# Three interaction layers of a recommendation tower: 24 of 39 fields multiplied in pairs, seven block products for eight

## The reference

```
prev = x
for k in 0, 1, 2:
    z = einsum('bmd,bhd->bdmh', x, prev)          # all products of a field and a unit
    t = einsum('bdc,co->bdo', z, w[k]) + b[k]     # 128 outputs
    t = t / sqrt(sum of t*t over outputs and d)   # one norm per sample
    logit.append(t); prev = t
z = sum over d of the three t                     # 384 numbers per sample
h = relu([z, dense] @ W_top1 + b_top1); h = relu(h @ W_top2 + b_top2); y = h @ W_top3
```

## Time and profile before

| | us |
|---|---|
| median of 3 runs (1243.51 to 1246.41) | 1246.39 |
| the profiled execution, its time | 1242.94 |
| its span, first to last instruction | 1240.9 |
| TensorE busy | 1201.1 |
| VectorE busy | 877.9 |
| GpSimd busy | 157.5 |
| ScalarE busy | 81.6 |

### The profile page before, as it was taken

One profiled execution on the slowest core, in us unless ns is written; L12 is line 12 of the kernel. 1 busy time (PEld: TensorE's weight loads), 2 busy tenths in 40 slices (PEclk: granted clock), 3 DMA queues, 4 the chain that ended last, 5 costly groups with the idle time before them and its releaser, 6 DMA issues.

```text
span 1240.9 us, 9676 instructions
## 1 busy us (share of the span) xinstructions
PE 1201.1 (97%) x2808; PEld 531.4 (43%) x2808; DVE 877.9 (71%) x748; ACT 81.6 (7%) x139; POOL 157.5 (13%) x183
## 2 busy tenths in 40 slices
PE   0899999999999999999999999999999999999999
PEld 0334444444444444444444444444444444444443
DVE  1657787677687777768678677867767876876671
ACT  0010010101001010000101000010100001010002
POOL 5130203020030301103030120303002030000000
PEclk9899999999999999999999999999999999999999
DMA  4988275461826647183563718356271745627000
GB/s 96 400 247 298 58 248 148 176 216 58 280 62 223 172 152 226 50 287 76 196 200 126 233 39 281 111 177 218 100 245 50 260 135 177 215 69 260 0 1 0
DMA packets 92574, 203.70 MB, mean 164 GB/s; under 512 B 41756, under 2 KB 49692, under 8 KB 92567
## 3 DMA queue, kind: packets, MB, share of 16 engines
q1 hardware_dynamic: 85786, 202.08, 49.6%
q0 software_dynamic: 5120, 1.29, 1.3%
q10 hardware_dynamic: 1660, 0.25, 0.1%
HBM read 201.67 MB, written 1.90 MB: 164 GB/s over the span
## 4 chain that ended last, share of the span: by engine, by line
PE 93%; SPq 4%; DMA 1%; POOL 1%; issue 1%; DVE 0%; ACT 0%; POOLq 0%
PE acc L464 84%; PE acc L448 7%; SPq L218 1%; SPq L188 1%; SPq L210 1%; POOL gathered L167 1%; PE t_ps L515 1%; SPq L203 1%; DMA xr<-xt 1%; DMA xt<-gathered 0%; PE acc L505 0%; PE nrm_ps L474 0%; DMA gathered<-in_table,rows_of 0%; SPq L190 0%; DMA base_sb<-in_base 0%
## 5 line engine op out<-in xcount | busy, mean ns | idle before, releaser
L464 PE MATMUL acc<-z,w_sb 128*128 128x512 f32 x2496 | 1079.6, 593 | 6.8 <-DVE z L353 6.7
L353 DVE TENSOR_TENSOR z<-t_ps,xb 128x1536 f32<-128x1536 f32 x416 | 709.0, 1752 | 227.8 <-PE acc L464 142.1
L464 PEld LDWEIGHTS acc<-z,w_sb 128*128 128x128 f32 x2496 | 473.5, 190 | 597.9 <-issue 571.4
L167 POOL DMA_INDIRECT gathered<-in_table,rows_of x160 | 152.8, 955 | 60.8 <-issue 47.8
L448 PE MATMUL acc<-xr,w_sb 117*128 117x512 f32 (+1 forms) x224 | 102.6, 609 | 29.3 <-issue 28.6
L161 POOL TENSOR_TENSOR rows_of<-ids_sb,base_sb 128x10 int32<-128x10 int32 x16 | 3.3, 205 | 795.4 <-DMA xt<-gathered 793.9
L339 DVE TENSOR_TENSOR xr<-x,xr 117x512 f32<-117x512 f32 (+1 forms) x112 | 69.0, 686 | 31.4 <-DMA x<-xt 18.3
L448 PEld LDWEIGHTS acc<-xr,w_sb 117*128 117x128 f32 (+1 forms) x224 | 43.3, 195 | 85.4 <-issue 82.9
L378 DVE RECIPROCAL inv<-root 128x96 f32<-128x96 f32 (+2 forms) x18 | 12.4, 687 | 60.9 <-ACT root L292 60.8
L280 ACT ACTIVATE t_ps<-acc,bias 128x512 f32<-128x512 f32 x16 | 10.6, 662 | 461.1 <-PE acc L464 421.2
L268 ACT ACTIVATE sq<-scaled,bias 128x512 f32<-128x512 f32 x16 | 11.6, 722 | 387.8 <-issue 268.8
(11 more groups left out here) (41 smaller groups left out, 53.6 us busy)
## 6 DMA issues: line engine op xcount, KB each, us to landing
xb<-xt SPq DMA_DIRECT2D x208, 768.0 KB, 6.3
xr<-xt SPq DMA_DIRECT2D x144, 156.0 KB
x<-xt SPq DMA_DIRECT2D x45, 78.0 KB
gathered<-in_table,rows_of POOLq DMA_INDIRECT x160
xr<-xt SPq DMA_DIRECT2D x32, 78.0 KB
w_sb<-in_w SPq DMA_DIRECT2D x13, 192.0 KB, 10.3
xt<-gathered SPq DMA_DIRECT2D x16, 72.0 KB, 6.9
wt_sb<-in_wt SPq DMA_DIRECT2D x1, 768.0 KB
```

Source lines behind the costliest of these rows:

```text
L167: nc.gpsimd.indirect_dma_start(gathered[0:n, g, :], None, table[:, :], bass.IndirectOffsetOnAxis(rows_of[0:n, g:g + 1], 0)).then_inc(rows_ ...
L353: nc.vector.tensor_tensor(z[:, s % ZSLOTS, :, :], fields_of(k), xb[:, c * CH:(c + 1) * CH, :], ALU.mult).then_inc(z_ready, 1)
L464: last = nc.tensor.matmul(acc[k][:, :], w_sb[k][:, m, :], z[:, s % ZSLOTS, r, :], start=(m == 0), stop=(m == FIELDS - 1))
```

## The change

Two fields a and b, whose weights are cut into left and right halves of outputs (64 each) and whose z is cut into two halves of columns (N1, N2, 256 each, samples 0 to 15 and 16 to 31 of the tile), form a 2x2 by 2x2 block product. Strassen's scheme (in Winograd's form) does it with seven block products of 128 rows, 64 outputs and 256 columns in place of eight, and with sums before and after. 24 of the 39 fields are paired (12 pairs, two pairs to a chunk "P" of 4 fields, 6 such chunks a layer); 15 stay direct, three to a chunk "D". A layer is D P P D P P D P P D D, 11 chunks. What changes:

- **TensorE.** Every matmul of layers 0 to 2 and of the norms has 64 outputs, LEFT (PSUM partitions 0 to 63) or RIGHT (64 to 127). A direct field is two of them with 512 columns. A P chunk is 14 blocks of 256 columns: 8 that need only z and weights, 2 that need the first sum, 4 that need the others. Three of the seven products go to accumulators shared by pairs (`mix_ps`, `p7_ps`). The order of a tile is as before, with `range(0, 5)` before `add_partitions` and `range(5, 11)` after it.
- **GpSimd.** Per P chunk three adds or subtracts of 128x512 (`pair_sums`), into two slots; per tile three of 128x48 (`mix_rows`), which form the sign-changed and mixed rows of x that the scheme needs (so z itself comes out already combined); the gathers are split 8 and 2 and stand behind the last P chunk of layers 1 and 2.
- **VectorE.** Products of 3 rows (D) or 4 rows (P), into a ring of 14 rows; four sums of weights per layer, once (`mixed_weights`); per layer and tile five sums of 64x256 (`shared_sums`) and an add to the accumulator (`add_shared`); layer 0's seven products in four instructions. `normalize` stands after chunk 4, `scale0` after chunk 5.
- **ScalarE.** Per layer three copies between partition halves (`carry`); layer 1's bias moves to VectorE.
- **SyncE.** The mixed rows go to DRAM (`xq`) and each P chunk of `xb` is two loads; w1 is loaded whole at the start; the dense layers' weights are loaded into `xb` at the end.

The core of the diff (the ring, semaphores, buffers and the adapted norms are left out):

```diff
+CHUNKS = [("D", 0), ("P", 0), ("P", 1), ("D", 1), ("P", 2), ("P", 3), ("D", 2), ("P", 4), ("P", 5), ("D", 3), ("D", 4)]
+LEFT, RIGHT = slice(0, UNITS // 2), slice(UNITS // 2, UNITS)
+N1, N2 = slice(0, H), slice(H, N)
...
+            def pair_sums(i, k, c):
...
+                b11, t3 = z[:, at:at + 2, N1], z[:, at:at + 2, N2]
+                b21, b22 = z[:, at + 2:at + 4, N1], z[:, at + 2:at + 4, N2]
+                t2, t4, t1 = (sums[:, n % SUM_SLOTS, r, :, :] for r in range(3))
+                pool.wait_ge(z_ready, chunks_to(i, k, c))
...
+                nc.gpsimd.tensor_tensor(t2, t3, b11, ALU.add).then_inc(sums_ready, 1)
+                pool.wait_ge(sums_ready, done + 1)
+                nc.gpsimd.tensor_tensor(t4, b21, t2, ALU.subtract).then_inc(sums_ready, 1)
+                nc.gpsimd.tensor_tensor(t1, b22, t2, ALU.subtract).then_inc(sums_ready, 1)
...
+            def tile(i, mix=True, gathers=True, last=False):
...
+                        pair_sums(i, k, c)
+                        if k == 1 and c == FIRST_P and mix:
+                            mix_rows(i + 1)
+                        if k == 1 and c == LAST_P and gathers:
+                            gather(i + 2, range(0, 8))
+                        if k == 2 and c == LAST_P and gathers:
+                            gather(i + 2, range(8, GROUPS))
...
+            def shared_sums(i, k):
...
+                dve.wait_ge(cross_ready, n + 1)
+                nc.vector.tensor_tensor(u2[RIGHT, :], cross[RIGHT, N2], mix_ps[RIGHT, N1], ALU.add).then_inc(v_step, 1)
+                dve.wait_ge(v_step, 5 * n + 1)
+                nc.vector.tensor_tensor(u2[RIGHT, :], u2[RIGHT, :], mix_ps[RIGHT, N2], ALU.add).then_inc(v_step, 1)
...
+            def add_shared(i, k):
...
+                dve.wait_ge(z_used, chunks_to(i, k, NCH - 1))
...
+                    nc.vector.scalar_tensor_tensor(raw12[:, :], acc[1][:, :], bias[:, 1:2], v[:, :],
+                                                   ALU.add, ALU.add).then_inc(v_used, 1)
...
             def tile(i, first=False, last=False):
-                for c in range(CHUNKS):
+                for c in range(NCH):
                     products(i, 1, c)
+                    if c == 0 and not first:
+                        shared_sums(i - 1, 2)
+                    if c == 1 and not first:
+                        add_shared(i - 1, 2)
+                    if c == 4 and not first:
+                        norm_sums(2, i - 1)
+                    if c == 6 and first:
+                        mixed_weights(2)
                 if not last:
-                    products0(i + 1)
-                for c in range(CHUNKS):
+                    products0(i + 1, (0, 1))
+                shared_sums(i, 1)
+                if not last:
+                    products0(i + 1, (2, 3))
+                add_shared(i, 1)
+                for c in range(NCH):
                     products(i, 2, c)
-                    if c == 2:
-                        sums(1, i)
-                    if c == 3 and not last:
-                        sums(0, i + 1)
-                    if c == 6:
+                    if c == 1:
+                        norm_sums(1, i)
+                    if c == 2 and not last:
+                        norm_sums(0, i + 1)
+                    if c == 4:
                         normalize(i + 1, *layers_of(first, last))
-                        if not last:
-                            scale0(i + 1)
+                    if c == 5 and not last:
+                        scale0(i + 1)
...
+            def direct(i, k, c):
...
+                for r in range(3):
+                    for o in (LEFT, RIGHT):
+                        last = nc.tensor.matmul(acc[k][o, :], w_sb[k][:, D_FIELD + 3 * d + r, o], z[:, at + r, :],
+                                                start=(c == 0 and r == 0), stop=(c == NCH - 1 and r == 2),
+                                                skip_group_check=True)
...
+            def pairs(i, k, c):
...
+                for r, (a, b) in enumerate(pair_fields(p)):
+                    s4 = s_sb[k][:, 2, 2 * p + r, :]
+                    block(acc[k], LEFT, N1, w_sb[k][:, b, LEFT], z[:, at + 2 + r, N1])
+                    block(mix_ps, RIGHT, N1, w_sb[k][:, a, LEFT], z[:, at + r, N1], first and r == 0, final and r == 1)
+                    block(acc[k], LEFT, N2, s4, z[:, at + 2 + r, N2])
+                    block(p7_ps, RIGHT, N1, w_sb[k][:, a, RIGHT], z[:, at + r, N2], first and r == 0, final and r == 1)
+                done = 3 * (2 * NP * i + n)
+                pe.wait_ge(sums_ready, done + 1)
+
+                block(mix_ps, LEFT, N2, s_sb[k][:, 1, 2 * p, :], sums[:, slot, 0, 0, :], first, final)
+                block(mix_ps, RIGHT, N2, s_sb[k][:, 1, 2 * p + 1, :], sums[:, slot, 0, 1, :], False, final)
+                pe.wait_ge(sums_ready, done + 3)
+                for r, (a, b) in enumerate(pair_fields(p)):
+                    block(mix_ps, LEFT, N1, s_sb[k][:, 0, 2 * p + r, :], sums[:, slot, 2, r, :], False, final and r == 1)
+                    last = block(acc[k], RIGHT, N1, w_sb[k][:, b, RIGHT], sums[:, slot, 1, r, :])
...
             def tile(i, first=False, last=False):
-                layer(i, 1, range(CHUNKS), first)
+                layer(i, 1, range(NCH), first)
                 if not last:
                     layer0(i + 1)
                 layer(i, 2, range(0, 5), first)
                 add_partitions(i + 1, *layers_of(first, last))
-                layer(i, 2, range(5, CHUNKS), first)
+                layer(i, 2, range(5, NCH), first)
```

More of the change, by code:

```diff
@@ L20 @@
 N = TILE_B * EMB
+H = N // 2
 GROUP = P // TILE_B
@@ L134, in build, with at_first, chunks_to, mix_no @@
         y_acc, y_ready, y_written = sem("y_acc"), sem("y_ready"), sem("y_written")
[L136 to L141, removed]
+        def at_first(i):
+            return isinstance(i, int) and i == 0
+        def chunks_to(i, k, c):
+            return STEPS * i + (k - 1) * NCH + c + 1
+        def mix_no(i, k):
+            return 2 * i + k - 1
         def layers_of(first=False, last=False):
@@ L175, in _ @@
+            gather(0, range(GROUPS))
+            mix_rows(0)
+            gather(1, range(GROUPS))
+            tile(0)
+            with pool.Fori(1, TILES - 2) as i:
+                tile(i)
+            tile(TILES - 2, gathers=False)
+            tile(TILES - 1, mix=False, gathers=False, last=True)
         @block.sync
@@ L237, in _ @@
+                for c in range(NCH):
+                    sp.wait_ge(z_ready, chunks_to(i - 1, 2, c))
+                    load_chunk(i, c)
             with sp.Fori(1, TILES - 1) as i:
@@ L442, in layer0 @@
             def layer0(i):
-                if not (isinstance(i, int) and i == 0):
+                if not at_first(i):
                     pe.wait_ge(raw_ready[0], i)
-                for k in range(STEPS0):
-                    n = WIDE if k < STEPS0 - 1 else NARROW
-                    pe.wait_ge(z0_ready, STEPS0 * i + k + 1)
-                    last = nc.tensor.matmul(acc[0][:, :], w0_sb[0:n, k, :], xr[0:n, k, :],
-                                            start=(k == 0), stop=(k == STEPS0 - 1))
@@ L462, in layer @@
-                    for r in range(CH):
-                        m = CH * c + r
-                        last = nc.tensor.matmul(acc[k][:, :], w_sb[k][:, m, :], z[:, s % ZSLOTS, r, :],
-                                                start=(m == 0), stop=(m == FIELDS - 1))
-                    last.then_inc(z_used, 1)
+                    if c == 0 and not at_first(i):
+                        if k == 1:
+                            pe.wait_ge(v_used, mix_no(i - 1, 1) + 1)
+                        else:
+                            pe.wait_ge(scaled_ready, i)
```

434 lines of the change are left out of this document (291 added, 143 removed).

## The result

The changed kernel took 1333.43 us (median of 4 runs, 1330.52 to 1336.59) against 1246.1 us before (4 runs), ratio 1.0706, 95% interval 1.0677 to 1.0736: slower by 7.1%. Forecast were 1307 us and a range of 1235 to 1480. The profiled execution has a span of 1330.5 us, 89.6 more than before.

A forecast was written before the change was run, and what follows sets the result against it. TensorE's matmuls were taken to bound the kernel at 73.19 us a tile. Matmuls 68.04, lag 1.9 and wait 7.0, less some 0.2, gave 76.7 a tile; with start and end +60 us, forecast 1307 us, range 1235 to 1480.

The forecast's parts named there:

- The first case: Layer 2's wait for normalize outweighs the saved eighth of matmuls: 1307 us, own range 1270 to 1350, chance 0.57.
- The saved matmuls: TensorE's 12 pair chunks a tile, halves side by side: 3.01 us for 3.44 each, 5.15 saved, 68.04 us a tile.
- The wait for normalize: TensorE idles 4.7 us before layer 2's chunk 5 each tile, plus 2.3 for a lowered clock: together 7.0 us.
- The halves' lag: Array halves run one pass apart, one idling at column-width changes and drains: nine passes of 0.215, 1.9 us a tile.
- GpSimd's sums: Three 512-column sums per pair chunk at 1.06 us each, mostly hidden behind the chunk before.
- The start: First tile: layer 1's savings cancel VectorE's wait for w2 (load ending about 63); layer 2 adds 5.3 us.
- The last tile with the tail: Layer 1 -1.7, bare wait for layer 2 +1.7, layer 2 +5.3, and 0.7 us behind the last matmul.
- Case 2: Saved matmuls decide if halves don't lag, clock stays up, sums take 0.53: 72.7 us a tile, 1235 us; chance 0.12.
- Case 4: GpSimd bounds: sums of 1.75 us give about 1500 us, sums of 1.4 give 1350; chance 0.06.
- Cases 3 and 5: 3: halves overlap but staggered starts pay loads, about 1485 us, chance 0.16; 5: no overlap, about 2360, chance 0.09.

The follow-up runs named there:

- the version with nothing in the way: The changed kernel in another order of work, with normalize's prod, half and rnorm held in PSUM and add_shared's first sum in raw12: 1187.9 us, ratio 0.9552.
- Two edits that remove the wait: Against the changed kernel: add_partitions moved from behind chunk 4 to behind chunk 2, 1263.5 us; or normalize moved from behind chunk 4 to behind chunk 6, 1253.2 us.
- the blocks of the kernel before: The kernel before, each matmul of layers 1 and 2 cut into four blocks of 64 outputs by 256 columns, no sums: 1262.2 us, ratio 1.0140.
- the first three: On the changed kernel: add_partitions behind chunk 2, 1263.5 us; normalize behind chunk 6, 1253.2 us; five useless matmuls put in TensorE's gap, 1342.1 us.
- the late weight sums: The changed kernel with add_partitions behind chunk 2, and layer 2's weights summed behind chunk 10's products in the first tile: 1261.0 us, ratio 1.0120.
- the reordered kernel: The changed kernel with late sums of layer 2's weights, add_partitions behind chunk 1, mix_rows later, gathers split five and five, write_mixed behind load_layer0: 1234.0 us.
- the first experiment: The changed kernel with add_partitions moved in TensorE's list from behind chunk 4 of layer 2 to behind chunk 2: 1263.5 us, ratio 1.0154.
- the two behind it: The reordered kernel with normalize behind chunk 5, 1242.0 us; then also with add_shared of layer 2 behind chunk 2 in place of 1, 1238.0 us.
- half sums: GpSimd's sums over 256 of 512 columns (outputs not the reference's): on the changed kernel 1282.4 us; with add_partitions behind chunk 2 as well, 1176.7 us.
- operands in PSUM: The reordered kernel with prod, half and rnorm in PSUM and add_shared's first sum in raw12: 1187.9 us; with add_shared behind chunk 2 as well, 1188.3 us.

## Why the prediction was right, and where its sizes were off

The first case came true: the wait that the new order makes outweighs the saved eighth.

- **The saved matmuls.** Forecast 68.04 us a tile on full overlap of the halves. Right: starts 0.01 us apart, chunks of 3.02 us (forecast 3.01), and 68.70 a tile in the version with nothing in the way. The bound taken from loads 0.11 us apart held. The Trainium skill's 2.38 times for three column tiles (TensorE: Matmul & The Clock Gate, Part 3, measured speedup) spoke against it. No run here has three tiles; two halves gave the full 2.
- **The wait for normalize.** Forecast 4.7 us, measured 4.62 in fourteen tiles and 4.15 and 4.14 in the first and the last. Forecast +2.3 for the clock; chunk 5 is longer by 2.7 in the tile shown (5.70 for 3.02) and by 2.5 in the mean. The size is right, the reason only half: at full clock late sums make it 2.2 longer, where the prediction had 1.1, so a clock that stayed up would have gained 0.3 us a tile at most. Two edits that remove the wait gained 70 and 80 us, not the full 7.3 x 16 = 117; some 30 us of the difference are a tile's waits for sums, which grew from 1.7 to some 3.5 us in both.
- **The halves' lag.** 1.9 us was the mis-sized term on the high side. The two halves go in lock-step, so none lags by a pass, and only drains and restarts are left: 77.91 - 68.04 - 4.62 - 2.7 - 1.7 = about 0.9 us. That this term was 1.0 too high and the waits for sums, next, were 1.7 too low is why the usual tile, 77.45 us, lies so near the forecast 76.7: that part is luck.
- **GpSimd's sums.** Mis-sized on the low side: 1.06 forecast, 1.28 measured, so three take 3.8 us where a chunk has 3.02. Two more places show it in each tile, 1.12 and 0.57 us, where I had none. "At 1.4 they begin to hold layer 1's second pair chunk" named the place; it begins at 1.28. The Trainium skill (GPSIMD Engine Reference, 3.1) gave an estimate of 1.12, 0.16 too low here.
- **Late gathers.** Not in the sum at all. Before, GpSimd was busy for 13% and a gather late by some us cost nothing. Now sums stand behind gathers, and four of fourteen tiles lost 2.6 to 5.2 us more than the usual 77.45. Together they lost 14 us; the rest by which fourteen tiles missed the forecast (78.47 - 76.7 = 1.8, x 14 = 25 us of the 29.5 that the span missed) is the usual tile's 0.75.
- **The start.** I let the first layer's savings and its wait for w2 cancel. They did not: VectorE's wait for w2 ended at 67.0, where the load was forecast to end at 63, TensorE waited 5.88 us, with a lowered clock behind it, and 0.87 and 0.55 us for sums. +10.8 against +5.3. The last tile with the tail: 4.8 against 6.0.
- **The rivals.** Case 2 wanted three things right at once. The halves' lag was near nothing; the clock did fall, and the sums were 1.28, not 0.53. No run meets all three, but with sums of 0.73 to 0.76 a tile is 75.15; less the 2.2 us that the low clock adds to chunk 5 there, an estimate of 72.95 lies by case 2's 72.7 and under the 73.19 of before. So its mechanism was sound and its conditions not met. Case 4's sums of 1.4 gave 1350 and the truth lies a little under, by its mechanism in small. Cases 3 and 5 are refuted by the blocks of the kernel before.

My expectations were too hopeful eight times. In the first three I let the sums fill in less than they did, for the blocks of the kernel before I had nothing for their small costs, and for the late weight sums the 4.35 us won at the start did not last. For the reordered kernel I priced VectorE's small instructions by rows in which GpSimd was idle, though the first experiment's trace already had half at 1.17 us (mean of 14); in the two behind it I knew the length and let its wait vanish by another place. With half sums, and with operands in PSUM, they were too gloomy, by 19, 19, 14 and 4 us. Open is what brings the clock down apart from the 4.62 us gap: it fell behind some waits of 1.9 us and not behind others.

## What to carry to other kernels

When chunks are regrouped, count again how many lie ready behind every instruction of an in-order list: the store that hid normalize was two chunks and became none, which cost more than the whole saving. Work moved to an idle engine brings that engine's other jobs and their hiccups onto the path, and it can slow a second engine that it never waits for; take durations for a forecast from rows where both are at work. Before an idea is dropped, take its suspected costs away one by one: here the same block products went from 7.1% slower to 4.5% faster.

## What the runs showed of the hardware

- Two float32 matmuls of 64 columns each, on the left and right half of the array, run fully side by side: a pass of 256 moving columns every 0.215 us on both.
- A VectorE instruction with both operands in SBUF and a GpSimd sum hold each other up: 0.26 us became 1.10 to 1.32, rnorm being 0.27 again with operands in PSUM, and prod, with one operand there in every run, 0.26 or 0.27 in all. Other marks of it: rows_of on GpSimd 0.2 us before and 1.07 (mean of 16) after, where it stands beside layer 0's products, which read both operands from SBUF, and a sum of 1.65 at 663.90 beside a VectorE scale. The Trainium skill (SBUF — State Buffer, Who interferes with whom) states it: a VectorE instruction with two SBUF inputs contends with a GpSimd instruction that reads SBUF, over a port pair that only one of them holds at a time. The traces agree, for half, rnorm and feat above all.
- Behind every wait of 4.62 us the granted clock falls to or near its 1.2 GHz level for part or all of the next chunk (0.51 to 0.73 over it, 0.55 over 5.87 us in the tile shown). Five matmuls on one half of the array in the gap kept it up (1.00 over 910.25 to 915.48), but in some tiles not past the wait of 1.9 us inside that chunk.
